# A two-layer perceiver block: the last network's weights clamped on POOL and cast in quarters, its first tile interleaved with the attention's last products

## The chip, the cores and the metric

The kernel runs on one core of a Trainium2 chip. Its engines each work through a queue of their own: TensorE (PE) multiplies, VectorE (DVE) and ScalarE (ACT) compute elementwise and read the accumulators, GpSimd (POOL) computes elementwise on SBUF, and SyncE (SP) issues the DMAs. They wait for each other through semaphores. The metric is the device time of one execution in microseconds.

## The reference, cut to what matters

Two layers follow each other, each with cross attention, self attention and a feed-forward network, all on x of 16 x 64 rows and 256 columns, with a residual sum and a layer norm ahead of each. The change touches the last two blocks, the second layer's self attention (16 heads of 128, rotary, causal, batch 4 of 256 rows) and its network in float8:

```python
def _L1_ffn_ref(x, w_gating, w_linear):
    ...
    def _qdot(x, w, out_dtype=BF16):
        return jnp.dot(x.astype(E4M3), w.astype(E4M3), preferred_element_type=out_dtype)
    ff_gate = _qdot(x, w_gating[0])
    gate_value = jax.nn.gelu(ff_gate)
    ff1 = _qdot(x, w_gating[1])
    activations = gate_value * ff1
    outputs = _qdot(activations, w_linear)
    return outputs
...
x = x + _L1_attn_ref(_layernorm(x, axis=-1), ...)
x = x + _L1_ffn_ref(_layernorm(x, axis=-1), L1_ffn_w_gating, L1_ffn_w_linear)
```

## The kernel before

x stays in SBUF as eight tiles (TILES) of 128 rows; TH = 4 tiles are one half, TP = 2 a pair. The self attention (`self_attention_rotary`) works in 32 units (UNITS): 16 heads (H) on the first half of the rows, then 16 on the second. Every engine runs `step(n)`, a pipeline over units: step n projects unit n (q, k and v), scores unit n - 1, turns and mixes (probabilities by v) unit n - 2, and adds unit n - 3 to the output. Steps 32 to 34 only drain it. On DVE a step is rope of q (L2179), the masked score (L2195), its minimum (L2199), rope of k, the reciprocal (L2218) and `z_lo` (L2222); on ACT the split of the weights of unit n + 2 (`w_hi`, L1739), the copy of the turned probabilities (L2131), the exponentials (L2137), v (L2144) and `z_hi` (L2150), the mixed values rounded to 16 bits, for which `z_lo` is the rest; on POOL the two rope sums (L2003), of which the second lets PE score the unit, the division of the probabilities (L2007) and `w_lo` (L1746); on PE the order is: project, score (L2064), project, turn (L2073), output (L2044), v, mix (L2095).

The network (`gated_ffn_steps`) needs three weights of 128 x 2048 (gate, up, down) in float8. SP loads them raw (`gf_raw`) in steps 20, 24 and 28. ACT casts each whole, with saturation, behind its steps 28, 29 and 30 (`cast_weight`, L1832). The norm ahead of the network (`normalise_steps`) is made in two halves: statistics (L83, L86, L89) on DVE, the reciprocal root on POOL (L95), the scale on DVE (L102), transposes on PE (L110), and on ACT the cast of two tiles (L1779). The first half's statistics stand in DVE's step 19 and its scale in step 28; its transposes come only behind step 33.

The network runs in twelve steps; in step i PE multiplies tile i by gate and up in two halves of 512 columns each, multiplies tile i - 3 by down, and transposes h of tile i - 2 into bank 4. DVE casts h of tile i - 3 out of that bank (L1855), copies the gate halves (L1861), multiplies gate by up for tile i - 1 (L1867) and adds tile i - 4 to x (L1871). ACT copies up (L1841), computes Gelu (L1843) and copies the down product (L1848). Each tile is stored as its add is done.

## Time and profile before

| what | value |
|---|---|
| three runs, median (lowest to highest) | 806.4 us (803.45 to 808.24) |
| the profiled execution | 809.39 us, its span 807.6 us |
| granted TensorE clock, mean over the span | 0.954 of full speed |
| PE, DVE, ACT, POOL busy over the span | 86%, 73%, 53%, 46% |
| end of the last DVE add, and of the span | 805.5 us, 807.6 us |

The span runs from the first instruction to the last; the time of an execution also holds what lies around it, 1.8 us here. Times in the rows below count from the span's start. The second layer's self attention starts at about 520 us and gives its last sum at 768.6 us, the network the rest. Busy shares are means over stages with different limits, so the rows of the last 120 us are to be read, not the shares.

### The profile page before, as it was taken

What the parts mean: (1) busy time and instruction counts of PE and PEld (TensorE: products, weight loads), DVE (VectorE), ACT (ScalarE), POOL (GpSimd) and SP (SyncE); (2) the same over time, 40 slices, a digit from 0 to 9 for tenths busy, and PEclk for the clock granted to TensorE, in tenths of its full rate; (3) what the DMA queues carried; (4) which work ended last, traced back from release to release, by engine and by line L of the source; (5) the groups of instructions that cost most, each with busy time, mean ns of one, the idle gap of its engine ahead of it and who ended that gap; (6) DMA issues with size and microseconds to landing.
All of it is one profiled execution on the core that took longest, in us unless ns stands there. A gap on an engine that the chain in (4) does not pass through costs nothing. (4 is left out here: it accounts for less than half of the span.)

```text
span 807.6 us, 16000 instructions
## 1 busy us (share of the span) xinstructions
PE 693.7 (86%) x5487; PEld 464.3 (57%) x5490; DVE 588.5 (73%) x1152; ACT 426.2 (53%) x1314; POOL 370.3 (46%) x313
## 2 busy tenths in 40 slices
PE   4998799889566669999995999779999999999786
PEld 3664566579324434344432677447777777777544
DVE  3366787766678746666575788798888898888577
ACT  1365789525257622222244788236555555559764
POOL 3500554347136404344485555256676676666200
PEclk9999899999869859999999999999999999999989
DMA  9445000000030030522010000012221233130001
GB/s 242 121 138 202 1 2 1 1 2 1 1 91 1 1 110 1 148 100 92 1 39 1 2 2 2 1 40 61 60 58 40 59 113 112 44 107 23 1 1 54
DMA packets 33572, 41.92 MB, mean 52 GB/s; under 512 B 15072, under 2 KB 23264, under 8 KB 32608
## 3 DMA queue, kind: packets, MB, share of 16 engines
q1 hardware_dynamic: 33504, 41.06, 17.1%
q8 instruction: 37, 0.61, 0.3%
q14 instruction: 31, 0.25, 0.1%
HBM read 40.00 MB, written 1.05 MB: 51 GB/s over the span
## 5 line engine op out<-in xcount | busy, mean ns | idle before, releaser
L2003 POOL TENSOR_TENSOR ra_direct<-ra_direct,ra_crossed 128x512 f32<-128x512 f32 x64 | 81.3, 1270 | 78.7 <-DVE ra_crossed L2179 78.5
L661 ACT ACTIVATE c_probs<-bank,c_neg_max 128x128 f32<-128x128 f32 x256 | 91.6, 388 | 26.3 <-DVE c_neg_max L740 26.3
L2179 DVE SCALAR_TENSOR_TENSOR ra_crossed<-bank,ra_bias,ra_sin 64x512 f32<-64x512 f32 x128 | 96.0, 750 | 1.9
L700 POOL TENSOR_TENSOR c_probs<-c_probs,c_inverse 128x512 f32<-128x512 f32 x64 | 66.7, 1043 | 63.1 <-DVE c_inverse L715 63.1
L1468 POOL TENSOR_TENSOR r_turned<-r_times_a,r_times_b 128x1024 f32<-128x1024 f32 x24 | 56.4, 2350 | 72.2 <-DVE r_times_b L1667 72.2
L661 ACT ACTIVATION_READ_ACCUMULATOR c_probs<-bank,c_neg_max 128x1 f32 x256 | 58.1, 227 | 0.0
L2131 ACT ACTIVATE ra_probs_t<-bank 64x256 f32<-64x256 f32 x64 | 24.2, 379 | 60.8 <-PE bank L2073 60.5
L1746 POOL TENSOR_TENSOR ra_w_lo<-ra_raw,ra_w_hi 128x768 f16<-128x768 f32 x32 | 52.7, 1647 | 0.0
L2137 ACT ACTIVATE ra_probs<-ra_masked,ra_neg_max 128x64 f32<-128x64 f32 x128 | 43.1, 338 | 17.2 <-DVE ra_neg_max L2199 17.1
L58 PE MATMUL bank<-xt_hi,ra_w_hi 128*128 128x512 f16 x128 | 49.3, 385 | 1.6 <-DVE ra_crossed L2179 0.9
L58 PE MATMUL bank<-xt_lo,ra_w_hi 128*128 128x512 f16 x128 | 48.9, 382 | 0.0
L58 PE MATMUL bank<-xt_hi,ra_w_lo 128*128 128x512 f16 x128 | 48.8, 381 | 0.0
L730 DVE COPY c_probs_t<-bank 128x512 f32<-128x512 f32 x64 | 43.9, 686 | 5.8 <-PE bank L601 5.7
L2179 DVE SCALAR_TENSOR_TENSOR ra_direct<-bank,ra_bias,ra_cos 128x512 f32<-128x512 f32 x64 | 47.6, 744 | 0.4 <-PE bank L58 0.3
L601 PEld LDWEIGHTS bank<-ident_sb,c_probs 128*128 128x128 f32 x256 | 28.7, 146 | 29.8 <-issue 21.9
L2222 DVE SCALAR_TENSOR_TENSOR ra_z_lo<-bank,ra_v_bias,ra_z_hi 128x512 f16<-128x512 f32 x32 | 23.9, 748 | 28.6 <-ACT ra_z_hi L2150 28.6
L58 PE MATMUL bank<-ra_w_hi,xt_hi 128*128 128x128 f16 x256 | 44.5, 219 | 0.0
L58 PE MATMUL bank<-ra_w_hi,xt_lo 128*128 128x128 f16 x256 | 44.5, 219 | 0.0
L58 PE MATMUL bank<-ra_w_lo,xt_hi 128*128 128x128 f16 x256 | 44.5, 219 | 0.0
L619 PE MATMUL bank<-c_probs_t,c_keys 128*64 128x512 f32 x128 | 34.8, 622 | 10.8 <-DVE c_probs_t L730 10.8
L740 DVE TENSOR_REDUCE c_neg_max<-bank 128x4 f32<-128x512 f32 x64 | 40.8, 678 | 2.5 <-PE bank L58 2.5
L58 PE MATMUL bank<-kvt_hi,l_q_stack 128*128 128x128 f16 x256 | 35.1, 231 | 7.5 <-PEq L1424 4.5
(271 smaller groups left out, 2092.5 us busy)
## 6 DMA issues: line engine op xcount, KB each, us to landing
ra_raw<-l_attn_w_dram SPq DMA_DIRECT2D x32, 384.0 KB, 3.1
wq<-l_wq_dram SPq DMA_DIRECT2D x16, 256.0 KB, 2.8
wo<-l_wo_dram SPq DMA_DIRECT2D x16, 256.0 KB, 3.2
wkcq<-l_wkcq_dram SPq DMA_DIRECT2D x16, 192.0 KB, 3.0
...
```

Of the source, the lines that this page charges most:

```text
L58: mm = nc.tensor.matmul(out, lhs, rhs, start=(n == 0), stop=(n == last))
L601: mm = nc.tensor.transpose(turn_bank[q][:, n, :], probs[u][:, q * HP + n, :], m.ident[:])
L619: mm = nc.tensor.matmul(mix_view[e * DC:(e + 1) * DC], keys[u][:], probs_t[u][:, :, e * S:(e + 1) * S], start=True, stop=True)
L661: e = nc.scalar.activation(probs[u][:, n, :], score_bank[u][q][:, n - q * HP, :], ACT.Exp, bias=neg_max[u][:, n:n + 1], accum_out=total[u] ...
L700: nc.gpsimd.tensor_tensor(out=probs[u][:, at, :], in0=probs[u][:, at, :], in1=inverse[u][:, at].unsqueeze(2).broadcast_to([P, HP, L]), op= ...
L730: nc.vector.tensor_copy(probs_t[u][:, at, :], turn_bank[q]).then_inc(turn_kept, 1)
L740: nc.vector.tensor_reduce(neg_max[u][:, at], score_bank[u][q], AX.X, ALU.max, negate=True).then_inc(maxed, 1)
L1468: nc.gpsimd.tensor_tensor(out=turned[k % 3][:], in0=times_a[k % 2][:], in1=times_b[k % 2][:], op=ALU.add).then_inc(rotated, 1)
L1746: nc.gpsimd.tensor_tensor(out=m.ra_w_lo[f][:], in0=m.ra_raw[f % 2][:], in1=m.ra_w_hi[f][:], op=ALU.subtract).then_inc(g.ra_split, 1)
L2003: nc.gpsimd.tensor_tensor(out=direct[e][k][:], in0=direct[e][k][:], in1=crossed[k][:], op=ALU.add).then_inc(roped, 1)
L2137: ins = nc.scalar.activation(probs[1 - e][:, t, :], masked[1 - e][:, t, :], ACT.Exp, bias=neg_max[1 - e][:, t:t + 1], scale=-1.0, accum_ou ...
L2179: ins = nc.vector.scalar_tensor_tensor(dst[out_lo:out_lo + rows].rearrange("p t (b s) -> p (t b) s", b=2), src[lo:lo + rows], bias[e][lo:l ...
```

## The change

- `cast_weight` is gone. POOL clamps each weight in place in quarters of 512 columns to the float8 range (`clamp_quarter`), one in each step 16 to 27 ahead of its rope sums, and ACT casts one quarter, without saturation (`cast_quarter`), at the end of each of these steps. SP's loads of the raw weights move to steps 8, 10 and 12. The second half of the attention is no longer a hardware loop in its middle.
- The transposes of the norm's first half stand ahead of step 32's score on PE, their casts (`ln.high`) ahead of step 32's copy on ACT. The first tile's products by gate and up stand behind step 32's mix and behind step 33's turn, step 33's output product behind its mix. ACT's first copy of up and DVE's two gate copies move into step 33.
- The norm's second half goes in two pairs of tiles, with semaphores in place of drains, and its statistics on DVE stand right behind the attention's last sums, ahead of the second tile's gate copies.
- In the network POOL adds down to x, not DVE. PE transposes ahead of the down product, and tiles 5 and 7 are transposed into bank 6. It has eleven steps.

```diff
+    def count(dve, t):
+        nc.vector.bn_stats(m.all_stats[:, t, :], m.x[:, t, :]).then_inc(counted, 1)
+
+    def aggregate(dve, t):
+        dve.wait_ge(counted, t + 1)
+        nc.vector.bn_aggr(m.all_moments[:, t, :], m.all_stats[:, t, :]).then_inc(aggregated, 1)
+
+    def variance(dve, q):
+        dve.wait_ge(aggregated, groups[q][1])
+        rows = slice(*groups[q])
+        nc.vector.tensor_scalar(m.all_var[:, rows], m.all_moments[:, rows, 1], LN_EPS, None,
+                                ALU.add).then_inc(moments_done, 1)
...
-    w8 = [sb("gate_w8", [P, CC, FFN], F8), sb("up_w8", [P, CC, FFN], F8), sb("down_w8", [P, FT, D], F8)]
+    all_w8 = sb("all_w8", [P, 3, FFN * D // P], F8)
+    w8 = [all_w8[:, k, :].rearrange("p (c n) -> p c n", c=c) for k, c in enumerate((CC, CC, FT))]
...
-    ln = normalise_steps(nc, g, "gf_ln", banks=(0, 1, 6, 7), store=store_x8)
+    ln = normalise_steps(nc, g, "gf_ln", banks=(0, 1, 6, 7), store=store_x8,
+                         groups=((0, TH), (TH, TH + 2), (TH + 2, TILES)))
...
-    h_bank = g.bank[4][:].bitcast(BF16).rearrange("p (c n) -> p c n", c=FT)
+    h_home = [6 if t > TH and t % 2 else 4 for t in range(TILES)]
+    h_bank = [g.bank[k][:].bitcast(BF16).rearrange("p (c n) -> p c n", c=FT) for k in h_home]
...
+    def products(pe, t, q):
+        cols = slice(q * 512, (q + 1) * 512)
+        if t == 0 and q == 0:
+            pe.wait_ge(cast, 12)
+            pe.wait_ge(ln.ready, 2)
+        if t == TH and q == 0:
+            pe.wait_ge(ln.ready, 4)
+        wait(pe, gate_kept, 2 * (t - 1) + q + 1)
+        accumulate(nc, gate_bank[q], [(x8[:, c, t, :], w8[0][:, c, cols]) for c in range(CC)]).then_inc(gated, 1)
+        wait(pe, up_kept, 2 * (t - 1) + q + 1)
+        accumulate(nc, up_bank[q], [(x8[:, c, t, :], w8[1][:, c, cols]) for c in range(CC)]).then_inc(upped, 1)
...
+            t = i - 2
+            pe.wait_ge(multiplied, 2 * t + 2)
+            wait(pe, h_kept, max((e + 1 for e in range(t) if h_home[e] == h_home[t]), default=0))
...
-    def cast_weight(act, k):
-        act.wait_ge(g.gf_loaded, 48)
-        nc.scalar.activation(w8[k][:].rearrange("p a b -> p (a b)"), m.gf_raw[:, k, :], ACT.Copy,
-                             saturate=True).then_inc(cast, 1)
+        if has(i, 3):
+            t = i - 3
+            pe.wait_ge(h_kept, t + 1)
+            wait(pe, down_kept, t)
+            accumulate(nc, down_bank, [(h8[t % 2][:, c, :], w8[2][:, c, :]) for c in range(FT)]).then_inc(down_done, 1)
+
+    def clamp_quarter(pool, k, q):
+        at = slice(q * QUARTER, (q + 1) * QUARTER)
+        pool.wait_ge(g.gf_loaded, 48)
+        nc.gpsimd.tensor_scalar(m.gf_raw[:, k, at], m.gf_raw[:, k, at], F8_MAX, -F8_MAX,
+                                ALU.min, ALU.max).then_inc(clamped, 1)
+
+    def cast_quarter(act, k, q):
+        at = slice(q * QUARTER, (q + 1) * QUARTER)
+        act.wait_ge(clamped, 4 * k + q + 1)
+        nc.scalar.activation(all_w8[:, k, at], m.gf_raw[:, k, at], ACT.Copy, saturate=False).then_inc(cast, 1)
+
+    def gpsimd(pool):
+        for q in (1, 2):
+            ln.rstd(pool, q)
+        for t in range(TILES):
+            pool.wait_ge(down_kept, t + 1)
+            nc.gpsimd.tensor_tensor(out=m.x[:, t, :], in0=m.x[:, t, :], in1=down[t % 2][:],
+                                    op=ALU.add).then_inc(added, 1)
+
+    def keep_up(act, t, q):
+        act.wait_ge(upped, 2 * t + q + 1)
+        wait(act, multiplied, 2 * (t - 2) + q + 1)
+        nc.scalar.activation(up[t % 2][:, q, :], up_bank[q], ACT.Copy).then_inc(up_kept, 1)
...
-        if has(i, 4):
-            dve.wait_ge(down_kept, i - 3)
-            nc.vector.tensor_tensor(m.x[:, i - 4, :], m.x[:, i - 4, :], down[u][:],
-                                    ALU.add).then_inc(added, 1)
...
-        FFN_LOADS = (H + 4, H + 8, H + 12)
...
+        FFN_LOADS = (8, 10, 12)
...
+                if isinstance(n, int) and H <= n < H + 12:
+                    ffn.clamp_quarter(pool, (n - H) // 4, f)
...
-            ffn.ln.rstd(pool, 1)
+            ffn.gpsimd(pool)
...
+                if isinstance(n, int) and n == UNITS:
+                    pe.wait_ge(crossing, 2 * UNITS)
+                    for k in range(2):
+                        ffn.ln.transpose(pe, k)
...
-                if out:
+                if isinstance(n, int) and n == UNITS + 1:
+                    ffn.products(pe, 0, 1)
+                elif out:
...
-            def begin_ffn():
-                for k in range(2):
-                    ffn.ln.transpose(pe, k)
-                pe.wait_ge(v_kept, UNITS)
-                pe.wait_ge(limited, UNITS)
-                ffn.tensor(pe, 0)
-
-            unit_loop(pe, step, begin_ffn)
-            pe.wait_ge(mix_kept, UNITS)
+                if isinstance(n, int) and n == UNITS:
+                    pe.wait_ge(v_kept, UNITS)
+                    pe.wait_ge(limited, UNITS)
+                    ffn.products(pe, 0, 0)
+                if isinstance(n, int) and n == UNITS + 1:
+                    output(n, e, half)
+
+            unit_loop(pe, step)
...
+                if isinstance(n, int) and n == UNITS:
+                    for k in range(2):
+                        ffn.ln.high(act, k)
...
+                if isinstance(n, int) and n == UNITS + 1:
+                    ffn.keep_up(act, 0, 0)
...
-                if isinstance(n, int) and UNITS - 4 <= n < UNITS - 1:
-                    ffn.cast_weight(act, n - UNITS + 4)
+                if isinstance(n, int) and H <= n < H + 12:
+                    ffn.cast_quarter(act, (n - H) // 4, f)
...
+            ffn.keep_up(act, 0, 1)
+            for q in range(2):
+                ffn.gelu(act, 0, q)
...
-                    ffn.ln.statistics(dve, 0)
+                    dve.wait_ge(added, TP)
+                    ffn.statistics(dve, range(TH))
+                    ffn.ln.variance(dve, 0)
...
+                if isinstance(n, int) and n == UNITS + 1:
+                    for q in range(2):
+                        ffn.keep_gate(dve, 0, q)
...
-            unit_loop(dve, step, lambda: ffn.vector(dve, 0))
+            unit_loop(dve, step)
+            for q in range(TP):
+                dve.wait_ge(added, TP + q + 1)
+                ffn.statistics(dve, range(TH + 2 * q, TH + 2 * q + 2))
+                ffn.ln.variance(dve, q + 1)
             for i in range(1, ffn.steps):
                 ffn.vector(dve, i)
                 if i == 1:
-                    ffn.ln.statistics(dve, 1)
-                if i == 2:
-                    ffn.ln.scale(dve, 1)
+                    for q in (1, 2):
+                        ffn.ln.scale(dve, q)
```

ACT at the end of the attention, before: the last units with the whole casts and what follows. `gf_x` is the network's cast input, `gf_up` the kept up half.

```order
L2150 ACTIVATE ra_z_hi<-bank,ra_v_bias 128x512
L1832 ACT_TABLE_LOAD
L1832 ACTIVATE gf_down_w<-gf_raw 128x2048
L2131 ACTIVATE ra_probs_t<-bank 64x4x64 x2
L2137 ACT_TABLE_LOAD
L2137 ACTIVATE ra_probs,ra_total<-ra_masked,ra_neg_max 128x64 x4
L2144 ACTIVATE ra_v<-bank 128x512
L2150 ACTIVATE ra_z_hi<-bank,ra_v_bias 128x512
L2131 ACTIVATE ra_probs_t<-bank 64x4x64 x2
```

The same place of ACT now:

```order
L2207 ACTIVATE ra_z_hi<-bank,ra_v_bias 128x512
L2186 ACTIVATE ra_probs_t<-bank 64x4x64 x2
L2194 ACTIVATE ra_probs,ra_total<-ra_masked,ra_neg_max 128x64 x4
L2201 ACTIVATE ra_v<-bank 128x512
L2207 ACTIVATE ra_z_hi<-bank,ra_v_bias 128x512
L1797 ACTIVATE gf_x<-bank 128x2x256 x2
L2186 ACTIVATE ra_probs_t<-bank 64x4x64 x2
```

The casts and both table loads beside each have left these steps, and the casts of x stand ahead of the copy. A quarter's cast in steps 16 to 27 reads `L1861 ACTIVATE gf_all_w<-gf_raw 128x512`, with no table load beside it.

DVE from the attention's last sums on, before:

```order
L1861 CAST gf_gate<-bank 128x512 x2
L2209 TENSOR_TENSOR x_res<-x_res,bank 128x512 x2
L1861 CAST gf_gate<-bank 128x512 x2
L1867 TENSOR_TENSOR gf_h<-gf_gate_act,gf_up 128x512 x2
L83 BN_STATS all_stats<-x_res 128x6 x4
L86 BN_AGGR all_moments<-all_stats 128x2 x4
L89 TENSOR_SCALAR all_var<-all_moments 128x4
L1861 CAST gf_gate<-bank 128x512 x2
L1867 TENSOR_TENSOR gf_h<-gf_gate_act,gf_up 128x512 x2
L102 TENSOR_SCALAR all_xn<-x_res,all_moments,all_rstd 128x256 x4
L1855 TENSOR_SCALAR gf_h<-bank 128x1024
```

And now:

```order
L2267 TENSOR_TENSOR x_res<-x_res,bank 128x512 x2
L94 BN_STATS all_stats<-x_res 128x6 x2
L98 BN_AGGR all_moments<-all_stats 128x2 x2
L103 TENSOR_SCALAR all_var<-all_moments 128x2
L94 BN_STATS all_stats<-x_res 128x6 x2
L98 BN_AGGR all_moments<-all_stats 128x2 x2
L103 TENSOR_SCALAR all_var<-all_moments 128x2
L1895 CAST gf_gate<-bank 128x512 x2
L1902 TENSOR_TENSOR gf_h<-gf_gate_act,gf_up 128x512 x2
L116 TENSOR_SCALAR all_xn<-x_res,all_moments,all_rstd 128x256 x4
L1895 CAST gf_gate<-bank 128x512 x2
```

The statistics moved ahead of the second tile's gate copies, and the scale ahead of the third's.

PE from step 32's mix on, now (before, both products of the first tile and the transposes stood behind step 33's mix, ahead of the last output product):

```order
L2149 MATMUL bank<-ra_probs_t,ra_v 128x128 x4
L58 MATMUL bank<-gf_all_w,gf_x 128x512 x4
L2125 MATMUL bank<-ident_sb,ra_probs 128x128 x2
L58 MATMUL bank<-gf_all_w,gf_x 128x512 x4
L2149 MATMUL bank<-ra_probs_t,ra_v 128x128 x4
L2092 MATMUL bank<-ra_wo_hi,ra_z_hi 128x256
```

The two halves of the first tile's products now lie around the turn.

## Rows read from the trace of the kernel before

**Rows 1.** Timeline of VectorE, the mask of one unit each: start, duration, engine, line

```profile
691.28 0.43 DVE L2195 SCALAR_TENSOR_TENSOR ra_masked<-bank,ra_mask 128x256 f32<-128x256 f32 x1
...
719.98 0.43 DVE L2195 SCALAR_TENSOR_TENSOR ra_masked<-bank,ra_mask 128x256 f32<-128x256 f32 x1
...
735.54 0.42 DVE L2195 SCALAR_TENSOR_TENSOR ra_masked<-bank,ra_mask 128x256 f32<-128x256 f32 x1
...
743.62 0.42 DVE L2195 SCALAR_TENSOR_TENSOR ra_masked<-bank,ra_mask 128x256 f32<-128x256 f32 x1
...
751.46 0.42 DVE L2195 SCALAR_TENSOR_TENSOR ra_masked<-bank,ra_mask 128x256 f32<-128x256 f32 x1
```

**Rows 2.** Timeline of ACT behind step 30

```profile
748.47 1.28 ACT L1832 ACT_TABLE_LOAD   x1
749.77 1.91 ACT L1832 ACTIVATE gf_down_w<-gf_raw 128x2048 fp8e4<-128x2048 f32 x1
...
752.36 1.28 ACT L2137 ACT_TABLE_LOAD   x1
```

**Rows 3.** Timeline of VectorE, steps 28 and 29; in brackets the idle time before it

```profile
730.17 2.43 DVE L102 TENSOR_SCALAR all_xn<-x_res,all_moments,all_rstd 128x256 f32<-128x256 f32 x4
...
739.46 0.18 DVE L2218 RECIPROCAL ra_inverse<-ra_total 128x4 f32<-128x4 f32 x1 [0.85 <-ACT ra_probs L2137]
```

**Rows 4.** Timeline of PE, steps 31, 32 and the network's start

```profile
748.09 0.73 PE L2064 MATMUL bank<-ra_direct 128*64 128x64 f32 x16 [0.85 <-POOL ra_direct L2003]
...
755.92 0.73 PE L2064 MATMUL bank<-ra_direct 128*64 128x64 f32 x16 [1.88 <-POOL ra_direct L2003]
...
765.29 0.59 PE L58 MATMUL bank<-gf_gate_w,gf_x 128*128 128x512 fp8e4 x2 [0.97 <-ACT gf_x L1779]
...
776.59 1.94 PE L110 MATMUL bank<-ident_sb,all_xn 128*128 128x128 f32 x8 [3.70 <-issue]
```

**Rows 5.** VectorE by line from 769 us on: busy, mean ns, idle before

```profile
L1855 DVE TENSOR_SCALAR gf_h<-bank 128x1024 fp8e4<-128x1024 bf16 x8 | 9.8, 1226 | 2.7 <-PE bank L1826 2.7
L1861 DVE CAST gf_gate<-bank 128x512 bf16<-128x512 f32 x14 | 9.1, 687 | 2.2 <-PE bank L58 2.2
...
L1871 DVE TENSOR_TENSOR x_res<-x_res,gf_down 128x256 f32<-128x256 f32 x8 | 3.4, 424 | 1.2 <-ACT gf_down L1848 1.2
...
L102 DVE TENSOR_SCALAR all_xn<-x_res,all_moments,all_rstd 128x256 f32<-128x256 f32 x4 | 1.4, 412 | 0.0
```

**Rows 6.** Timeline of VectorE, step 33, the last sums, and two tiles

```profile
764.21 0.75 DVE L2222 SCALAR_TENSOR_TENSOR ra_z_lo<-bank,ra_v_bias,ra_z_hi 128x512 f16<-128x512 f32 x1 [3.19 <-ACT ra_z_hi L2150]
...
768.60 1.29 DVE L2209 TENSOR_TENSOR x_res<-x_res,bank 128x512 f32<-128x512 f32 x2 [1.12 <-PE bank L2044]
...
789.63 0.42 DVE L1871 TENSOR_TENSOR x_res<-x_res,gf_down 128x256 f32<-128x256 f32 x1
789.96 1.22 DVE L1855 TENSOR_SCALAR gf_h<-bank 128x1024 fp8e4<-128x1024 bf16 x1
...
793.29 1.23 DVE L1855 TENSOR_SCALAR gf_h<-bank 128x1024 fp8e4<-128x1024 bf16 x1
```

**Rows 7.** ACT and POOL by line, the whole span: busy, mean ns, idle before

```profile
L2131 ACT ACTIVATE ra_probs_t<-bank 64x256 f32<-64x256 f32 x64 | 24.2, 379 | 60.8 <-PE bank L2073 60.5
...
L338 POOL TENSOR_SCALAR l_raw_ffn<-l_raw_ffn 128x2048 f32<-128x2048 f32 x3 | 5.7, 1899 | 0.2
```

**Rows 8.** Timeline of POOL, the two rope sums of unit 28

```profile
727.12 1.28 POOL L2003 TENSOR_TENSOR ra_direct<-ra_direct,ra_crossed 128x512 f32<-128x512 f32 x1 [0.54 <-DVE ra_crossed L2179]
730.21 1.26 POOL L2003 TENSOR_TENSOR ra_direct<-ra_direct,ra_crossed 128x512 f32<-128x512 f32 x1 [1.82 <-DVE ra_crossed L2179]
```

**Rows 9.** PE in a slice of 1 us: length, busy (count), granted clock, DMA

```profile
775.00:776.00 1.00, 0.00 (x0) 0.50 0.00 0
```

**Rows 10.** Timeline of PE, two earlier instructions behind long pauses

```profile
271.20 0.62 PE L1267 MATMUL bank<-ident_h_sb,tf_h_int 128*128 128x128 bf16 x8 [2.76 <-DVE tf_h_int L1372]
...
536.49 1.17 PE L2064 MATMUL bank<-ra_direct 128*64 128x64 f32 x16 [2.90 <-POOL ra_direct L2003]
```

107 lines of the change are left out of this document (47 added, 60 removed).

## The prediction, made before the changed kernel had run

> **What bounds the kernel now.** I read the page first, then the starts of one VectorE instruction per unit, then the ACT, PE and POOL rows of the last units, then VectorE alone in the last network. Only the last 120 us are touched, so I look at what ends last there.
>
> In the middle of the second half the units start evenly: L2195 stands at 691.28 and four units later at 719.98, that is 7.18 us each [rows 1], and PE has no pause. Around units 29 to 31 this breaks: 735.54 to 743.62 is 8.08 us, 743.62 to 751.46 is 7.84 us [rows 1]. The cause is in ACT's rows: each long weight cast brings a table load of 1.28 us, the cast itself (1.91 us) and one more table load before the next exponentials [rows 2], 4.5 us of new work three times in an engine that in a plain unit has some 2 us to spare [rows 7]. VectorE then waits for the exponentials [rows 3], and PE waits for the rope that VectorE and POOL hand on: 0.85 us at 748.09 and 1.88 us at 755.92 [rows 4]. ACT is therefore the late one in three units, though its busy share is low.
>
> From 755.92 to the final attention sum at 768.60 [rows 4, 6] the last three steps are a chain from PE to ACT to VectorE and back. Into it, ahead of the last output product, come the eight transposes of the norm, a wait of 0.97 us for the cast of x, and the first tile's products [rows 4].
>
> Behind it VectorE is the bound: from 768.60 to its last add it idles 2.7 + 2.2 + 1.2 us [rows 5]; a tile takes the 3.33 us between two starts of L1855, 0.33 us of it the add of L1871 [rows 6].
>
> **Part 1, the weight casts.** Removed: three casts and six table loads, 3 x 1.91 + 6 x 1.28 = 13.4 us of ACT in units 28 to 31 [rows 2]. Added, in units 16 to 27: twelve casts of 512 columns. A quarter of 1.91 us is 0.48 us; with a fixed part I take 0.6 us, as one like it (the cast of x, 512 columns, no table load in the order of the changed kernel either). No row shows a plain cast of the weights by itself; its bounds are 0.5 and 0.8 us. It stands behind z_hi and delays only w_hi, which POOL needs a step later, and then L2131, before which ACT waits 60.5 us for PE in 32 units, 1.9 us in each [rows 7]. Cost 0. POOL's clamp: L338 takes 1.90 us for 2048 columns [rows 7], so about 0.5 us for 512; the upper bound is the two-input add of 512 columns, 1.27 us [rows 8]. It fits where POOL idles: 0.54 us before the first rope add and 1.82 us before the second [rows 8]. Only the second lets PE go on, so up to about 2.3 us of clamp cost nothing. Cost 0, and if that cover were gone its excess would be paid twelve times. The loads move on SP's queue from the second half to steps 8, 10 and 12, each behind the three transfers of its step, as before; 0.
>
> What is regained: the scale of four tiles on VectorE (2.43 us in unit 28 [rows 3]) stays, so the late start of unit 29 stays. From there VectorE, no longer waiting for ACT, goes rope, z_lo, rope, mask at its own pace. Unit 30's score would start at PE's own pace (1.0 us earlier than 748.09). Then the last rope: 2.25 + 0.65 + 2.25 + 0.85 + 2.25 us of VectorE work behind 742.8 and POOL's 1.27 us end at about 753.9 instead of 755.9. **Gain 2.0 us**; bounds 1.2 and 2.5 (the sum of the two excesses, 0.91 and 0.67, is 1.6).
>
> **Part 2, the first tile among the attention's last products.** The transposes move into PE's pause before the last score: PE would be done with unit 31 at 752.9, so they end at 753.9, just as the rope does. The first half of the products goes behind the mix of step 32, where PE waited for POOL's norm; the second half (0.86 us) behind the turn of step 33, and there it runs while ACT copies the turned probabilities, for which the mix waits anyway. ACT's two casts of x come ahead of its copy in step 32, in the time that the removed casts give back. Two gate casts, 1.2 us of VectorE, come ahead of its z_lo in step 33; VectorE idled 3.19 us there [rows 6]. Chain by chain: score 753.9, turn 754.6, output and mix to 757.3, z_hi and z_lo to 758.7, turn, products and mix to 760.3, z_hi 761.0, z_lo 761.7, last output 763.0; the adds of L2209 could start at 763.1. Before, 755.92 to 768.60 took 12.7 us; now 753.9 to 763.1 takes 9.2. **Gain 3.5 us**. The upper bound is all that left the path, 1.0 transposes + 0.97 wait + 1.73 products = 3.7; the lower one 2.0, if the new rows ahead of the copies and z_lo each arrive late.
>
> **Part 3, the network's tiles.** VectorE from its first add on, in work: adds 1.2, statistics 2.2 and, for twice the waits on its own results, 0.3 (bounds 0 and 0.6: a reduction that waited so in L2199 starts some 0.1 us later than one that did not); then gates, products, scale (1.4 [rows 5]), and eight casts of h. A tile loses the add: 3.33 - 0.33 = 3.0 us [rows 6]. But PE needs about 3.05 us a tile at the full clock, so I take 3.07 for the four steady tiles. POOL's add (half of 1.27 us for half the columns, 0.64 us [rows 8]) hides behind the next tile in all but the last, where it replaces 0.42 us: +0.2. At the end, h has a second bank for its transposes and they no longer stand behind the down product, so VectorE goes from one cast of h to the next: the waits of 0.59 and 1.26 us before L1855, 1.85 of the 2.7 [rows 5], go. What is late next is the chain down, ACT, add, of 2.0 us, as before.
>
> Now the clock. Before, PE pauses 3.70 us for the norm's second half [rows 4]; in the slice from 775 it is granted 0.50, the 1.2 GHz level [rows 9], and the eight transposes behind the pause take 1.94 us [rows 4]. With that VectorE idled 3.0 us over three waits. The change shortens the pause but does not remove it: products of tile 2 wait for gate casts of tile 1, and these now stand behind the statistics of all four tiles. PE is through with tile 1 at 1.75 us after the last output, the first gate cast ends at 4.4: a pause of 2.7 us. One of 2.76 us at 271.20 left the clock whole (0.62 us for eight transposes); one of 2.90 us did not: the score product behind it took 1.17 us instead of 0.73 [rows 4, 10]. I take the fall, since the pause lies with little work on either side: about 4 us of PE work take twice as long, VectorE waits some 1.1 us at tile 3 and in all 1.4 us instead of 3.0. Part 3 is then 2.3 (seven adds) + 1.85 + 1.6 - 0.2 (POOL's last) - 0.3 - 0.05 = **5.2 us**; 6.6 if the clock holds, 3.6 if it costs the 3.0 us of before.
>
> **Two rules.** The scale of four tiles took 2.43 us in unit 28, with a rope add of POOL beside it [rows 8], and 1.4 us in the network with POOL idle [rows 3, 5]. The Trainium skill, "SBUF — State Buffer", section "Who interferes with whom", says that VectorE and GpSimd share a port pair as an exclusive lock, also between a VectorE instruction with two SBUF inputs and a reading GpSimd one. By that rule, the trace agrees, POOL's adds could stop VectorE's product of gate and up; the third rival works this out. ACT's table load took 1.28 us and its next instruction began at once [rows 2]. The Trainium skill, "ScalarE: Activation LUTs", section "What ACT_TABLE_LOAD costs", puts a switch at 2.66 us with a drain; by that figure the casts would have taken 21.7 us of ACT; no such drain lies between the rows here.
>
> **The sum.** 2.0 + 3.5 + 5.2 = 10.7 us. The profiled execution took 809.39 us with a span of 807.6; it would be 798.7. It lies 3 us above the median of three, 806.4, so I forecast 806.4 - 10.7 = **795.7 us**. A measurement can tell about 0.5%, 4 us, from no change.
>
> **Rivals.**
> (1) The clock holds through the pause: 12.1 us, **794.3**. For it speaks the pause of 2.76 us, against it that of 2.90 [rows 10]. 25%.
> (2) The last steps give less: the new rows ahead of copy and z_lo arrive late and PE and VectorE, now both near 3.05 us a tile, hinder each other, by up to the add's 0.33 us in six tiles. 1.2 + 2.0 + 5.2 - 2.0 = 6.4 us: **800.0**. Against it: ACT has idle time in every tile. 15%.
> (3) POOL's add meets the gate-up product each tile. Blocked by 0.64 us in six steady tiles is 3.8 us: 10.7 - 3.8 = 6.9, **799.5**. Against it: the add should come while VectorE casts h from PSUM, over a microsecond before the product. 7%.
> (4) The clamp outgrows POOL's idle time, and the kernel ends slower. From 2.3 us on, each microsecond more costs twelve in units 16 to 27; 3.4 us a clamp gives +13 - 10.7, **809**. Against it: the dearest near row, 1.27 us [rows 8]. 2%. That the casts still load tables is excluded: the order has no table load beside them.
> The forecast itself holds 51%.
>
> **Range.** The parts' lower bounds give 1.2 + 2.0 + 3.6 = 6.8 us, the upper 2.5 + 3.7 + 6.9 = 13.1, so 793.3 to 799.6; the three runs of before spread by 2.4 us around their median, which I add in part: **791.0 to 801.0**. Faster by over 0.5% is all but part of (2), (3) and all of (4): 0.93; within 0.5% 0.04; slower 0.03.
>
> **What would show it.** Units 29 to 31 start 7.2 to 7.5 us apart, with no table load in ACT between 530 us and the first Gelu. The clamps take about 0.5 us and units 16 to 27 keep their 7.18 us. From the score of step 32 to the first of the last attention adds it is about 9.2 us. VectorE's h casts in steady tiles start 3.0 to 3.1 us apart, the last three 1.2 us apart with hardly a wait. One pause of PE near 2.7 us, with or without a stretch of 0.50 behind it. I am wrong if a plain quarter costs ACT over 2 us, if z_lo of step 33 waits for the gate casts, or if tiles stay at 3.33 us.

## The result, and the profile after

| | changed kernel | kernel before | ratio (95% interval) |
|---|---|---|---|
| first measurement, median (lowest to highest) | 795.42 us (791.49 to 803.73) | 804.92 us (801.41 to 808.24) | 0.9861 (0.9817 to 0.9905) |
| measured once more | 796.66 us (791.13 to 797.56) | 807.24 us (802.25 to 812.21) | 0.985 (0.978 to 0.992) |

The forecast was 795.7 us. The kernel is about 1.4% faster, and the sum of the prediction holds to within what a median can tell; its terms don't all hold, and they are what the rest is about. The run of 803.73 us, over 1.5% above the fastest of its kernel, is left out of the ratio but not out of the median.

Whole times are a blunt tool here. The profiled execution of the changed kernel is that one of 803.73 us. As in the prediction, "unit n" stands for the mask in step n; the first, VectorE's L2253 of unit 1, begins the second layer's attention. It stands at 535.19 us in that profile and at 528.39 in the one of the repetition, of the same code; over all fourteen profiles of this case it lies between 524.3 and 538.6 us, and no edit touches what comes before. Behind it a stage that an edit leaves alone repeats to some hundredths of a microsecond (A, B) or to about 0.2 (M, C), wherever no DMA is waited for. So I compare stages, each between two starts on the timelines: **E**, masks of units 4 to 18; **M**, 18 to 28; **A**, mask of unit 28 to step 32's score; **B**, from there to the first of the attention's last adds; **C**, to the end of the last add to x. The last column is the whole way from the mask of unit 1 to that end.

| us | E | M | A | B | C | unit 1 to end |
|---|---|---|---|---|---|---|
| before | 100.63 | 72.93 | 28.85 | 12.68 | 36.87 | 273.46 |
| changed | 102.01 | 72.76 | 27.08 | 9.93 | 31.02 | 264.55 |
| changed, repeated | 101.39 | 72.78 | 27.08 | 9.94 | 31.00 | 265.19 |

A gained 1.77 us (forecast 2.0), B 2.75 (3.5), C 5.85 (5.2): 10.4 in place of 10.7. E lost 0.8 to 1.4 us, for which the prediction has no term; over the eight profiles here and below that have the same loads and no more clamps it is 0.1 to 1.6, against a single profile of before. Units 1 to 4 are in no stage; with the same code up to there they took 21.75 us in the first profile and 23.00 in the repetition.

**Units and casts.** VectorE's masks of units 29 and 30 [rows 1] (unit 28's is at 731.71, unit 31's at 754.32):

```profile
740.18 0.42 DVE L2253 SCALAR_TENSOR_TENSOR ra_masked<-bank,ra_mask 128x256 f32<-128x256 f32 x1
...
746.73 0.42 DVE L2253 SCALAR_TENSOR_TENSOR ra_masked<-bank,ra_mask 128x256 f32<-128x256 f32 x1
```

The 8.47 us of unit 28 stays, as the scale of four tiles stays; the 8.08 of the next is 6.55 now, and the 7.84 of the one behind it 7.59. The new work by line, on ACT (behind 640 us) and on POOL (behind 520 us): busy, mean ns, idle before:

```profile
L1861 ACT ACTIVATE gf_all_w<-gf_raw 128x512 fp8e4<-128x512 f32 x12 | 7.4, 620 | 0.0
```

```profile
L1855 POOL TENSOR_SCALAR gf_raw<-gf_raw 128x512 f32<-128x512 f32 x12 | 7.4, 614 | 0.1
L1868 POOL TENSOR_TENSOR x_res<-x_res,gf_down 128x256 f32<-128x256 f32 x8 | 5.3, 668 | 21.5 <-ACT gf_down L1890 21.5
```

A quarter's cast is 0.62 us (0.6 was taken), a clamp 0.61 (about 0.5), POOL's add 0.67 (0.64). The casts have no table load beside them. M shows that they cost nothing there: 72.76 against 72.93 us.

**The first tile.** Timeline of PE from the transposes of step 32 on; L58 with `gf_x` is a half of the first tile's products [rows 4]:

```profile
757.60 1.04 PE L124 MATMUL bank<-ident_sb,all_xn 128*128 128x128 f32 x8
758.79 0.73 PE L2116 MATMUL bank<-ra_direct 128*64 128x64 f32 x16 [0.15 <-POOL ra_direct L2051]
...
761.93 1.03 PE L58 MATMUL bank<-gf_all_w,gf_x 128*128 128x512 fp8e4 x4
763.11 0.44 PE L2125 MATMUL bank<-ident_sb,ra_probs 128*128 128x128 f32 x2 [0.15 <-POOL ra_probs L2055]
763.38 1.03 PE L58 MATMUL bank<-gf_all_w,gf_x 128*128 128x512 fp8e4 x4
```

and of VectorE beside it [rows 6]:

```profile
763.56 1.28 DVE L1895 CAST gf_gate<-bank 128x512 bf16<-128x512 f32 x2
766.32 0.75 DVE L2285 SCALAR_TENSOR_TENSOR ra_z_lo<-bank,ra_v_bias,ra_z_hi 128x512 f16<-128x512 f32 x1 [1.48 <-ACT ra_z_hi L2207]
768.72 1.29 DVE L2267 TENSOR_TENSOR x_res<-x_res,bank 128x512 f32<-128x512 f32 x2 [1.65 <-PE bank L2092]
```

The pauses of PE before the score and the turn are 0.15 us each (1.88 and 0.78 before): the moved work fills them. The last z_lo still waits 1.48 us for ACT behind the two gate casts, so those are in nobody's way.

**The network.** VectorE by line from the last sums on [rows 5]:

```profile
L1910 DVE TENSOR_SCALAR gf_h<-bank 128x1024 fp8e4<-128x1024 bf16 x8 | 9.6, 1216 | 0.0
L1895 DVE CAST gf_gate<-bank 128x512 bf16<-128x512 f32 x14 | 9.3, 686 | 0.1
L1902 DVE TENSOR_TENSOR gf_h<-gf_gate_act,gf_up 128x512 bf16<-128x512 bf16 x16 | 6.3, 438 | 0.0
```

Before, the last column held 2.7, 2.2 and 1.2 us; now VectorE hardly waits from its first add to its last cast of h, although PE pauses 2.48 us and the clock falls. Timeline of PE, then PE in slices of 1 us: length, busy (count), granted clock [rows 9]:

```profile
772.81 3.35 PE L58 MATMUL bank<-gf_all_w,gf_x 128*128 128x512 fp8e4 x8 [2.48 <-DVE gf_gate L1895]
```

```profile
772.00:773.00 1.00, 0.19 (x1) 1.00 0.00 0
773.00:774.00 1.00, 1.00 (x4) 0.55 0.00 0
...
776.00:777.00 1.00, 1.00 (x12) 0.74 0.00 0
```

The tile's products, 1.89 us elsewhere, take 3.35 at 0.50 (1.2 GHz), which lasts from 773.1 to 776.5 or so. Steady tiles and the end, on VectorE:

```profile
783.37 1.22 DVE L1910 TENSOR_SCALAR gf_h<-bank 128x1024 fp8e4<-128x1024 bf16 x1
784.51 1.33 DVE L1895 CAST gf_gate<-bank 128x512 bf16<-128x512 f32 x2
785.75 0.75 DVE L1902 TENSOR_TENSOR gf_h<-gf_gate_act,gf_up 128x512 bf16<-128x512 bf16 x2
786.42 1.22 DVE L1910 TENSOR_SCALAR gf_h<-bank 128x1024 fp8e4<-128x1024 bf16 x1
...
793.64 1.09 DVE L1902 TENSOR_TENSOR gf_h<-gf_gate_act,gf_up 128x512 bf16<-128x512 bf16 x2
794.66 2.34 DVE L1910 TENSOR_SCALAR gf_h<-bank 128x1024 fp8e4<-128x1024 bf16 x2
```

A tile is 3.05 us, and neither VectorE nor PE waits in it. The last two casts of h follow without a pause. The last pair of products takes 1.09 us instead of 0.75, in both profiles; POOL's add begins just before it:

```profile
793.45 0.67 POOL L1868 TENSOR_TENSOR x_res<-x_res,gf_down 128x256 f32<-128x256 f32 x1 [2.38 <-ACT gf_down L1890]
```

### The profile page after: what moved, and what is told of

It reads as the page before. It is cut to its first block and busy times, and to the rows that moved or that the text cites. A ratio compares the mean times of both kernels' runs of the same rounds, so it can differ in the third digit from the quotient of the medians.

```text
span 801.9 us, 15926 instructions
## 1 busy us (share of the span) xinstructions
PE 701.0 (87%) x5487; PEld 469.4 (59%) x5490; DVE 585.5 (73%) x1145; ACT 419.7 (52%) x1317; POOL 382.5 (48%) x334
## 3 DMA queue, kind: packets, MB, share of 16 engines
HBM read 40.00 MB, written 1.05 MB: 51 GB/s over the span
## 5 line engine op out<-in xcount | busy, mean ns | idle before, releaser
L58 PE MATMUL bank<-xt_hi,ra_w_hi 128*128 128x512 f16 x128 | 49.5, 387 | 1.2 <-PEq L577 0.8
L58 PE MATMUL bank<-xt_hi,ra_w_lo 128*128 128x512 f16 x128 | 49.3, 385 | 0.0
L58 PE MATMUL bank<-xt_lo,ra_w_hi 128*128 128x512 f16 x128 | 49.3, 385 | 0.0
L616 PEld LDWEIGHTS bank<-ident_sb,c_probs 128*128 128x128 f32 x256 | 28.7, 146 | 29.9 <-issue 21.1
L58 PE MATMUL bank<-ra_w_hi,xt_hi 128*128 128x128 f16 x256 | 45.4, 221 | 0.0
L58 PE MATMUL bank<-ra_w_lo,xt_hi 128*128 128x128 f16 x256 | 45.3, 221 | 0.0
L58 PE MATMUL bank<-ra_w_hi,xt_lo 128*128 128x128 f16 x256 | 45.2, 221 | 0.0
L58 PE MATMUL bank<-kvt_hi,l_q_stack 128*128 128x128 f16 x256 | 35.0, 231 | 7.5 <-PEq L1439 4.5
```

What stands on the lines that cost most here:

```text
L58: mm = nc.tensor.matmul(out, lhs, rhs, start=(n == 0), stop=(n == last))
L616: mm = nc.tensor.transpose(turn_bank[q][:, n, :], probs[u][:, q * HP + n, :], m.ident[:])
```

## The experiments

Theory: each part gives what its term says. The rivals differ by part and stand with each run. All of them are the changed kernel with the edit shown, but for the sixth. Stages in us.

| run | E | A | B | C | unit 1 to end |
|---|---|---|---|---|---|
| changed (both profiles) | 102.0, 101.4 | 27.08 | 9.93 | 31.01 | 264.6, 265.2 |
| whole casts, saturating | 101.63 | 28.04 | 9.99 | 31.00 | 265.19 |
| whole casts, plain | 102.22 | 27.09 | 9.94 | 30.94 | 264.81 |
| add on VectorE | 101.13 | 27.08 | 9.93 | 31.91 | 264.73 |
| one bank for h | 100.77 | 27.09 | 9.93 | 33.39 | 265.46 |
| first tile not interleaved | 101.98 | 27.07 | 12.44 | 30.82 | 266.50 |
| before, with early loads | 100.96 | 28.77 | 12.67 | 35.82 | 272.90 |
| clamp four times | 103.56 | 27.08 | 9.94 | 30.80 | 270.08 |
| clamp seven times | 107.38 | 28.96 | 9.93 | 31.01 | 293.62 |
| v bias loaded first | 100.48 | 27.08 | 9.92 | 31.01 | 263.03 |
| norm spread over units | 100.61 | 25.78 | 9.93 | 31.01 | 262.21 |
| more POOL work in the network | 101.31 | 27.08 | 9.93 | 37.00 | 269.99 |

**Whole casts, with saturation and without.** The first brings back the three whole casts of before and leaves the clamps out; the second keeps the clamps, waits for `clamped` at 4 * k + 4 and casts whole with `saturate=False`. The diff is the first's.

```diff
+    def cast_weight(act, k):
+        act.wait_ge(g.gf_loaded, 48)
+        nc.scalar.activation(all_w8[:, k, :], m.gf_raw[:, k, :], ACT.Copy, saturate=True).then_inc(cast, 1)
...
-                if isinstance(n, int) and H <= n < H + 12:
-                    ffn.cast_quarter(act, (n - H) // 4, f)
+                if isinstance(n, int) and UNITS - 4 <= n < UNITS - 1:
+                    ffn.cast_weight(act, n - UNITS + 4)
```

> The changed kernel with the weight casts as before: no clamp on POOL, three whole saturating casts on ACT behind steps 28, 29 and 30; all else stays. Stages are read from the trace: A from the mask of unit 28 to the last score, B from there to the first of the last attention sums, C from there to the end of the last add. Before: A 28.85, B 12.68, C 36.87 us; changed: 27.08, 9.93, 31.02. My theory (ACT is late there because of casts and table loads): A goes back to 28.8, B and C stay. Rival (A was shorter for another reason, the straight-line code or the drains): A stays at 27.1. Time 1.8 us over the changed kernel.

> The changed kernel with POOL's quarter clamps kept in steps 16 to 27, but the casts whole and plain (without saturation) behind steps 28, 29 and 30. It tells the length of the cast from its table loads. Theory: without saturation there is no table load, a cast costs ACT 1.9 us, about as much as ACT has to spare in a unit, and stage A (mask of unit 28 to last score) stays at 27.1 to 27.5 us. Rival (the cast's own length makes ACT late): A 28.3 or more.

Measured: A 28.04 us with saturation, 27.09 without; times 800.63 us (ratio to before 0.9898, 0.9827 to 0.9969) and 801.4 us (one run). ACT by line and on its timeline, saturating:

```profile
L1865 ACT ACT_TABLE_LOAD x3 | 3.8, 1283 | 0.1
```

```profile
733.17 1.28 ACT L1865 ACT_TABLE_LOAD   x1
734.46 1.91 ACT L1865 ACTIVATE gf_all_w<-gf_raw 128x2048 fp8e4<-128x2048 f32 x1
...
737.05 1.28 ACT L2196 ACT_TABLE_LOAD   x1
```

and plain:

```profile
741.38 1.91 ACT L1865 ACTIVATE gf_all_w<-gf_raw 128x2048 fp8e4<-128x2048 f32 x1
744.79 0.77 ACT L2190 ACTIVATE ra_probs_t<-bank 64x256 f32<-64x256 f32 x2 [1.50 <-PE bank L2129]
```

The plain cast is as long as the saturating one, and yet ACT waits 1.50 us for PE behind it: it costs nothing even in one piece. What made ACT late were the six table loads, which belong to the saturating form alone. The quarters as such give nothing; leaving out the saturation does. The table loads account for 0.96 of A's 1.77 us. The other 0.8 us lie in one unit, 8.08 us before and 7.26 in the saturating run. Timeline of ACT before, step 28:

```profile
731.37 0.69 ACT L2150 ACTIVATE ra_z_hi<-bank,ra_v_bias 128x512 f16<-128x512 f32 x1 [1.17 <-DMA ra_v_bias<-l_attn_bv_dram]
```

It makes z_hi start 4.30 us behind the mask of unit 28 instead of 3.48 in the saturating run. ACT has no slack there, with the casts and table loads behind z_hi, and the mask of unit 30 is late by the same 0.82 us. This wait for the bias of v is in both profiles with the old loop (1.09 us in the sixth run), where the load takes 3.4 and 3.3 us to land, and in none with the new one, where it takes 2.2 to 2.6 in the ten profiles that issue it in the same place. Why it lands late there no run tells; it stays open.

**The add on VectorE.**

```diff
-        for t in range(TILES):
-            pool.wait_ge(down_kept, t + 1)
-            nc.gpsimd.tensor_tensor(out=m.x[:, t, :], in0=m.x[:, t, :], in1=down[t % 2][:],
-                                    op=ALU.add).then_inc(added, 1)
...
+        if has(i, 4):
+            dve.wait_ge(down_kept, i - 3)
+            nc.vector.tensor_tensor(m.x[:, i - 4, :], m.x[:, i - 4, :], down[i % 2][:],
+                                    ALU.add).then_inc(added, 1)
```

> The changed kernel with the add of down back on VectorE, as before, in a twelfth step. Theory: VectorE is the bound of the tiles, a tile goes from 3.05 back to 3.33 us, C grows by about 2 us to 33.0. Rival (PE alone holds the tiles at 3.05 us, the add is free on VectorE): C stays at 31.0. Rival of the shared port (POOL's add slows VectorE in the changed kernel): C would grow by less than 1 us.

Measured: 802.64 us (0.9885, 0.9806 to 0.9964), C 31.91, only 0.90 us more where about 2 was expected. Timeline of VectorE at the end:

```profile
802.89 0.42 DVE L1915 TENSOR_TENSOR x_res<-x_res,gf_down 128x256 f32<-128x256 f32 x1 [1.17 <-ACT gf_down L1886]
```

A tile is 3.33 us again, but only four of them are bound by VectorE: counted from the first add, its sixth cast of h starts 1.19 us later. The adds behind it bring only 0.33 more up to the eighth, and from there to the end it is 0.63 us shorter, 0.25 of it in the last add, 0.42 instead of 0.67.

0.90 is also what the expectation's last rival allowed for, POOL's adds slowing VectorE in the changed kernel. They do, a little. Without them the pair of gate casts takes 1.27 us instead of 1.33 in the steady tiles, and the last pair of products 0.75 instead of 1.09. The first costs nothing that shows: the next run has the pair at 1.28 us and its tiles at 3.05 all the same. The second is 0.34 us, once.

**One bank for h, and the old order.**

```diff
-    h_home = [6 if t > TH and t % 2 else 4 for t in range(TILES)]
+    h_home = [4] * TILES
```

and in `tensor` the down product stands ahead of the transposes again. Bank and order are undone together; which of them gives how much no run tells.

> The changed kernel with bank 4 alone for the transposes of h and the down product ahead of them, as before. Theory: the last three tiles wait for each other again, C grows by 1.2 to 1.9 us, and the waits before VectorE's last two casts of h are 0.6 and 1.3 us. In the steady tiles nothing changes. Rival (POOL's add and the shorter VectorE step alone shortened the end): C stays within 0.4 us of 31.0.

Measured: C 33.39, 2.38 us more, beyond the expected 1.2 to 1.9 (795.32 us, one run). VectorE by line, and its last two casts:

```profile
L1910 DVE TENSOR_SCALAR gf_h<-bank 128x1024 fp8e4<-128x1024 bf16 x8 | 9.8, 1223 | 2.7 <-PE bank L1848 2.7
```

```profile
784.97 1.22 DVE L1910 TENSOR_SCALAR gf_h<-bank 128x1024 fp8e4<-128x1024 bf16 x1 [0.74 <-PE bank L1848]
787.78 1.22 DVE L1910 TENSOR_SCALAR gf_h<-bank 128x1024 fp8e4<-128x1024 bf16 x1 [1.59 <-PE bank L1848]
```

The waits of the drain come back, now 0.74 and 1.59 us where they were 0.59 and 1.26, since no add lies between; a third, of 0.39 us, stands before the third cast of h.

**The first tile not interleaved.** The transposes, both products, the casts of x, the gate and up copies go back behind step 33's mix; all else stays.

```diff
-                if isinstance(n, int) and n == UNITS + 1:
-                    ffn.products(pe, 0, 1)
-                elif out:
+                if isinstance(n, int) and n == UNITS + 2:
+                    for k in range(2):
+                        ffn.ln.transpose(pe, k)
+                    ffn.products(pe, 0, 0)
+                    ffn.products(pe, 0, 1)
+                if out:
```

> The changed kernel with the first tile as before: transposes, both products, casts of x, gate copies all ahead of the last output product or behind it, not in steps 32 and 33. Theory: B goes back to 12.5, A and C stay, time +2.6 us. Rival (B is shorter because ACT, rid of the casts, is on time): B stays near 10. PE should idle 0.8 us before step 33's turn and about 1 us for the cast of x again.

Measured: 801.22 us (0.9895, 0.9802 to 0.9987); B 12.44, 2.51 us more, within 0.24 of before. Timeline of PE (output products between the rows left out):

```profile
751.02 0.73 PE L2112 MATMUL bank<-ra_direct 128*64 128x64 f32 x16 [1.02 <-POOL ra_direct L2051]
...
755.34 0.44 PE L2121 MATMUL bank<-ident_sb,ra_probs 128*128 128x128 f32 x2 [1.02 <-POOL ra_probs L2055]
...
760.16 1.89 PE L58 MATMUL bank<-gf_all_w,gf_x 128*128 128x512 fp8e4 x8 [0.97 <-ACT gf_x L1797]
```

Transposes, the 0.97 us for x and the products are on the path again, and in return PE pauses 1.02 us before the score and before the turn. The interleaving is what B's gain consists of.

**Before, with early loads.** The kernel before with the one line on the loads.

```diff
-        FFN_LOADS = (H + 4, H + 8, H + 12)
+        FFN_LOADS = (8, 10, 12)
```

> The kernel before with only the raw weights' loads moved from steps 20, 24 and 28 to 8, 10 and 12. In the changed kernel's profile two units there were 1.5 and 0.9 us long, each with ACT waiting for the DMA of the v bias; units 4 to 18 took 102.0 us instead of 100.6. Theory 1 (the megabyte load, issued right behind the v bias, delays its landing): 102 us here too, with waits of ACT for the v bias beside the loads. Rival (that DMA is late now and then by chance, since it is issued only 3 us ahead of its use): 100.6 to 101, or waits at other steps.

Measured: 814.17 us in its one run, beside one of 802.86 us for the kernel before. Of this difference the stages hold nothing: its unit 1 to end is 0.56 us shorter. E is 0.33 us longer, where the theory had 102 us and the rival 100.6 to 101. The waits for the bias of v do stand beside the loads, as the theory had it: units 7 to 8 and 9 to 10 take 7.77 and 7.91 us, but others are shorter. A second reading came with it. PE's pause of 3.69 us is that of before (3.70), but C is 35.82 us and not 36.87. Slices of PE there; its last sums start at 774.43:

```profile
782.00:783.00 1.00, 0.59 (x3) 0.55 0.00 0
...
785.00:786.00 1.00, 1.00 (x5) 0.74 0.00 0
```

and of the kernel before, whose last sums start at 768.60:

```profile
781.00:782.00 1.00, 1.00 (x6) 0.60 0.00 0
```

Here the clock falls at about 782.1, shortly before PE takes up its work at 782.41, and is low for some 3.4 us. Before, it had fallen already in the pause [rows 9] and stayed low from 775 to nearly 782, some 6.8 us. VectorE waits 3.0 us in all over the three waits there before, and 1.95 here: C is 1.05 us longer by the only difference that I see. When the clock falls within a pause is not settled by the code alone.

**The clamp four and seven times.** The diff is of four times; seven differs by the number alone. The quarter's cast waits for the last clamp of its quarter.

```diff
-        nc.gpsimd.tensor_scalar(m.gf_raw[:, k, at], m.gf_raw[:, k, at], F8_MAX, -F8_MAX,
-                                ALU.min, ALU.max).then_inc(clamped, 1)
+        for r in range(4):
+            if r:
+                pool.wait_ge(clamped, 4 * (4 * k + q) + r)
+            nc.gpsimd.tensor_scalar(m.gf_raw[:, k, at], m.gf_raw[:, k, at], F8_MAX, -F8_MAX,
+                                    ALU.min, ALU.max).then_inc(clamped, 1)
```

> The changed kernel with every quarter clamped four times in a row on POOL, so about 2.2 us instead of 0.54 in each of units 16 to 27. Prediction's fourth rival: up to some 2.3 us cost nothing. Theory: units 20 to 28 keep 7.2 us each, at most 0.2 us more. Rival (POOL is already close to the path, every added 1 us shows): 8.8 us a unit, 12 x 1.6 = 20 us in all.

> As the one with four, but seven clamps, about 3.9 us. Theory: POOL's work in a unit is then 1.27 x 2 + 0.61 + 1.65 + 3.9 = 8.7 us and becomes the bound, units of about 8.7 to 8.9 us, 12 x 1.6 = 19 us more in all. Rival (POOL runs beside VectorE without ever being waited for): 7.2 us.

Measured: 803.71 and 824.55 us (one run each), unit 1 to end 5.2 and 28.8 us more than the mean of the changed kernel's two. Timeline of POOL in one unit, seven times:

```profile
685.59 4.79 POOL L1858 TENSOR_SCALAR gf_raw<-gf_raw 128x512 f32<-128x512 f32 x7
690.34 2.48 POOL L2054 TENSOR_TENSOR ra_direct<-ra_direct,ra_crossed 128x512 f32<-128x512 f32 x2
692.78 0.61 POOL L2058 TENSOR_TENSOR ra_probs<-ra_probs,ra_inverse 128x256 f32<-128x256 f32 x1
693.35 1.64 POOL L1761 TENSOR_TENSOR ra_w_lo<-ra_raw,ra_w_hi 128x768 f16<-128x768 f32 x1
694.96 4.79 POOL L1858 TENSOR_SCALAR gf_raw<-gf_raw 128x512 f32<-128x512 f32 x7
```

POOL has no pause and sets the unit: 9.37 us between two clamps, against 7.18 (8.7 to 8.9 were expected; seven clamps take 4.79 us and not 3.9). With four (2.71 us) a unit in the middle takes 7.3 us; most of the loss lies in units 17, 18 and 21, which became 1.4, 2.5 and 1.0 us longer, more than the expectation's 0.2. Why just these no run tells. In sum the idle time is what the prediction made of it, 2.3 us a unit: twelve times the excess over it is 4.9 us for four clamps and 29.9 for seven, beside the 5.2 and 28.8 measured. One clamp of 0.61 us uses a quarter of it.

**The bias of v loaded first.** In each of SP's steps the small load of the bias of v for unit n - 5 stands ahead of the others, and so ahead of the raw weights' wait for POOL. It is issued a whole step, some 7 us, sooner than in the changed kernel, not the 3 us of the expectation.

```diff
+                if 2 <= n - 5 < UNITS:
+                    load_v_bias(n - 5)
```

> The changed kernel with one move on SP's queue: in each step the v bias is issued first, ahead of the raw weights and the bias, so that it no longer stands behind the wait for POOL's w_lo. It is then issued about 3 us sooner. Theory: ACT never waits for this DMA in the attention (3.3 us in units 4 to 18 of the changed kernel's profile), units 4 to 18 take 100.4 to 100.7 us, and unit 28 to 29 loses its wait too. Rival (the wait is only moved, since PE and VectorE are as late): no change in the units' starts.

Measured: 797.0 us (one run); E 100.48 instead of 102.0 and 101.4, and unit 1 to end 263.03, the shortest but one. The next run, with the same edit, has E at 100.61; eight profiles without it, those with the repeated clamps left out, lie between 100.77 and 102.22. In the changed kernel SP issues, and ACT waits (its timeline below SP's):

```profile
579.74 0.33 SPq L2016 DMA_DIRECT2D ra_v_bias<-l_attn_bv_dram  x1
580.12 0.42 SPq L1814 DMA_DIRECT2D gf_raw<-l_up_dram  x1
```

```profile
583.40 0.69 ACT L2207 ACTIVATE ra_z_hi<-bank,ra_v_bias 128x512 f16<-128x512 f32 x1 [1.48 <-DMA ra_v_bias<-l_attn_bv_dram]
```

The 1 MB load is issued 0.38 us behind the small one, which lands late, after 3.6 us. In the eleven profiles with loads in steps 8, 10 and 12 and the old order, a small load with such a load right behind it lands after 2.3 to 3.7 us, 3.1 in the mean of 33; in the steps between and up to unit 15 it is 2.2 to 2.7. ACT's z_hi waits for this DMA 3.7 us in all in the changed kernel, 2.7 before, and here not at all, by line:

```profile
L2207 ACT ACTIVATE ra_z_hi<-bank,ra_v_bias 128x512 f16<-128x512 f32 x32 | 22.0, 687 | 10.1 <-PE bank L2149 10.1
```

This is E's loss: units 5 to 6, 7 to 8 and 9 to 10, those of the moved loads, take 7.71, 8.70 and 8.05 us where 7.2 is usual, and the ones behind them win only part of it back. The cure is the early issue, not a place away from the 1 MB load. With the edit the small load of the next step is issued right behind that load, and SP's timeline and the answer on this one transfer read:

```profile
559.26 0.42 SPq L1814 DMA_DIRECT2D gf_raw<-l_gate_dram  x1
559.77 0.38 SPq L2016 DMA_DIRECT2D ra_v_bias<-l_attn_bv_dram  x1
```

```profile
DMA to landing us min/median/max: 7.2/7.2/7.2
```

It lands after 7.2 us, the other two such after 6.6 and 7.1, and nobody waits, since it is needed later still.

**The norm spread over the units.** The edit above, and the first half's statistics and scale one tile per step instead of four in one.

```diff
-                    ffn.statistics(dve, range(TH))
...
-                if isinstance(n, int) and n == UNITS - 4:
-                    ffn.ln.scale(dve, 0)
+                if isinstance(n, int) and H + 3 <= n < H + 3 + TH:
+                    ffn.statistics(dve, range(n - H - 3, n - H - 2))
+                if isinstance(n, int) and UNITS - 8 <= n < UNITS - 8 + TH:
+                    ffn.ln.scale_tile(dve, 0, n - UNITS + 8)
```

> A version meant to beat both: the v bias issued first, and the norm's first half spread over the units: one tile's statistics in each of steps 19 to 22, one tile's scale in each of steps 24 to 27, in place of four at once in steps 19 and 28. Theory: VectorE has about 1 us to spare in a unit, so the two late units (19 to 20 by 0.8 us, 28 to 29 by 1.3 us) go; with the v bias about 2.5 to 3.5 us below the changed kernel, near 792 us. Rival (PE's queue gives no more, VectorE's slack is used up by waits): within 0.5 us of the changed kernel.

> The changed kernel once more, beside the others on the same chip: stages A 27.1, B 9.9 and C 31.0 us again, units 4 to 18 between 100.4 and 102 us; the TensorE clock falls or holds in the pause before tile 2, and C tells what that costs.

Measured: 799.81 us (0.9888, 0.9826 to 0.995), the changed kernel beside it 796.66 us (0.985, 0.978 to 0.992). The intervals overlap; neither is shown faster, and the expected time near 792 didn't come. By stages it is the shortest, 262.21 us, 2.3 and 3.0 under the changed kernel's two; E holds 1.4 and 0.8 of that, by the v bias. The spreading itself gave 1.3 us in A and 1.1 from unit 19 to 20 and lost 1.65 between units 20 and 28, 1.3 of it in units 24 to 27. Timelines of VectorE and POOL show why:

```profile
716.97 1.46 DVE L121 TENSOR_SCALAR all_xn<-x_res,all_moments,all_rstd 128x256 f32<-128x256 f32 x1
```

```profile
717.02 1.26 POOL L2057 TENSOR_TENSOR ra_direct<-ra_direct,ra_crossed 128x512 f32<-128x512 f32 x1 [1.83 <-DVE ra_crossed L2243]
```

Each of the four scales starts together with a rope add of POOL and takes 1.46 us, 5.8 in all, where four in a row take 2.43 beside such an add [rows 3] and 1.4 with POOL idle [rows 5]. The add makes VectorE wait some 1.1 us once; spread, this is paid four times.

**More POOL work in the network.** Behind its adds of tiles 1 to 4 POOL makes two adds of 512 columns on weights nobody reads any more.

```diff
+            if 0 < t < 5:
+                for r in range(2):
+                    if t > 1 or r:
+                        pool.wait_ge(padded, 2 * (t - 1) + r)
+                    nc.gpsimd.tensor_tensor(out=pad[:], in0=m.gf_raw[:, 0, 0:PAD], in1=m.gf_raw[:, 1, 0:PAD],
+                                            op=ALU.add).then_inc(padded, 1)
```

> The changed kernel with two more POOL additions of 512 columns behind the add of tiles 1 to 4, on data that nothing uses, so that POOL reads SBUF for about 2.5 us more in each tile and overlaps VectorE's product of gate and up. It measures the prediction's third rival. Theory (both read SBUF through one port): the products in tiles where POOL is at work take longer than their 0.42 us, up to 1.3 us, and the tiles grow by 0.5 us or more. Rival (no shared port for this instruction): 0.42 us each, tiles at 3.05 us.

Measured: 808.39 us (one run); C 37.00, 6.0 us more. POOL idled 2.38 us between two adds and the two new ones take 2.7, so a part of this is POOL's own lateness; the four pairs of products that meet them are 4.4 us longer in sum. VectorE's product and what POOL does beside it:

```profile
784.43 2.18 DVE L1910 TENSOR_TENSOR gf_h<-gf_gate_act,gf_up 128x512 bf16<-128x512 bf16 x2
```

```profile
783.61 2.71 POOL L1876 TENSOR_TENSOR gf_pad<-gf_raw 128x512 f32<-128x512 f32 x2
```

The pair of products takes 2.18 us instead of 0.75 while POOL reads. So the third rival's mechanism is real. In the changed kernel's steady tiles it doesn't occur, because POOL's add (0.67 us, at 784.31) lies beside the end of a cast of h and the gate casts, both from the accumulators, and the product at 785.75 keeps its 0.75 us. Only the last pair, at 793.64, meets an add. The Trainium skill, "SBUF — State Buffer", section "Who interferes with whom", says that a VectorE instruction with two inputs in SBUF contends with a GpSimd instruction that reads SBUF; the runs bear it out.

## Why the prediction was right, point by point

**The sum, 10.7 us.** The two measurements give 9.5 and 10.6 us between the medians, the way from unit 1 to the end 8.9 and 8.3. Parts 1 and 2 fell short by 1.0 us together, part 3 gave 0.65 more, and the loads lost what nobody had forecast. That the first median lies 0.3 us from the forecast is luck: the forecast went down from 806.4 us, and the kernel before then measured 804.92.

**Part 1, 2.0 us: 1.77.** The size came, but the working doesn't give it: 742.8 plus 8.25 us of VectorE's work and POOL's 1.27 is 752.3, not 753.9, and by it the gain would be 3.6 us. The cause is right in part. The prediction laid all of it to ACT's load, casts and table loads alike; the table loads are 0.96 us of it, the casts nothing, and 0.8 us was a wait for a DMA in step 28 that the prediction didn't see. The units came 6.55, 7.59 and 5.34 us apart, not 7.2 to 7.5. That clamp and quarter casts cost nothing held, with M and two multiplied clamps behind it.

**The loads, 0: wrong, 0.8 to 1.4 us lost.** The prediction looked at SP's queue alone ("each behind the three transfers of its step, as before"). The step that failed is this: the transfer in front of it, the bias of v, is needed 3 us later, and with a load of 1 MB right behind it takes 3.1 us to land in the mean, 3.7 at most, where the steps between have 2.5. Issued a step sooner, it keeps nobody waiting, and E is 100.48 us. In the kernel before the same move cost 0.33 us only, and E's loss in the profiles goes with the landings: 1.4 us where they took 3.3, 3.6 and 3.2 us, 0.1 in the run with one bank, where they took 3.2, 2.3 and 2.7.

**Part 2, 3.5 us: 2.75.** The interleaving is worth 2.5 us by the run without it. The order on each engine came as forecast, and no new row was late. Mis-sized was the chain: it was added up from durations, and from score to first add it is 9.93 us and not 9.2, since hand-overs between engines (0.26 us before the last output product, 0.15 before score and turn) were priced at nothing. Its lower bound of 2.0 held it.

**Part 3, 5.2 us: 5.85, by terms that are off in both directions.**

| term | forecast | measured |
|---|---|---|
| adds leave VectorE, POOL's last one dearer, tiles 3.05 | 2.05 | 0.9 |
| second bank and order for h | 1.85 | 2.4 |
| pause and clock, VectorE's idle time | 1.6 | 2.9 |
| twice the waits on own results | -0.3 | about 0 |

The measured terms come from single undoings and from the idle columns, and add up to 6.2, 0.35 more than C's gain; they aren't independent. The adds were counted seven times: four tiles bring 1.2 us, one add in the drain 0.3, and the end takes 0.6 back. The third term hangs on one profile of before. In the sixth run the clock was low half as long behind the same pause; against its C of 35.82 us the gain of part 3 is 4.8 and this term some 1.8. The forecast of 5.2 lies between, and neither shows it too low. The last three casts of h start 2.15 and 1.13 us apart, not 1.2 each: the last pair of products lies between, longer by POOL's add. For the clock: the pause (2.7 forecast, 2.48 measured) and the fall behind it came as forecast, but of the 1.4 us of waiting that it was to cost none is to be seen. VectorE had the scale (1.38 us) and a pair of products to do while PE was slow, and the cast of h that follows starts with no wait. The statistics in pairs took 2.15 us, so the doubled waits cost nothing.

**The rivals.** (1) The clock didn't hold, in none of the twelve profiles that have this pause of 2.48 us; yet the benefit that this rival promised came, because VectorE didn't wait. (2) Late rows: none. (3) The collision occurred in the last tile alone, for 0.34 us, and the added POOL work shows what it costs where it is met each tile. (4) The clamp is far from the limit; the limit itself is right.
